# Moving VectorE's second operands into PSUM, two jobs to GpSimd, and a new order of jobs, in a one-core attention and mixture-of-experts kernel

## The reference

```python
xn = layernorm(x)
uv = silu(xn @ uv_w); u, v = split(uv)
s = (u * toeplitz_convolution(v, filter_from_a_small_network)) @ o_w
rw = softmax(mean over tokens of xn @ Wr + br)          # one row for each sequence
w, e = softmax(top_2(rw))                               # 2 of 8 experts for each sequence
out = sum_j w_j * (gelu(xn @ W1[e_j] + b1[e_j]) @ W2[e_j] + b2[e_j])
g = silu(layernorm(out + xn) * gamma + beta)
x = x + s * g
```

## Time and profile before

| | us |
|---|---|
| median of 3 runs | 209.76 (209.5 to 209.9) |
| profiled execution, time | 209.87 |
| profiled execution, span from first to last instruction | 207.9 |
| TensorE busy in the span | 180.2 (87%) |
| VectorE, ScalarE, GpSimd busy | 158.2, 126.2, 139.8 |

### The profile page before, as it was taken

One profiled execution on the slowest core, in us unless ns is written; L12 is line 12 of the kernel. 1 busy time (PEld: TensorE's weight loads), 2 busy tenths in 40 slices (PEclk: granted clock), 3 DMA queues, 4 the chain that ended last, 5 costly groups with the idle time before them and its releaser, 6 DMA issues.

```text
span 207.9 us, 3882 instructions
## 1 busy us (share of the span) xinstructions
PE 180.2 (87%) x1167; PEld 159.5 (77%) x1167; DVE 158.2 (76%) x430; ACT 126.2 (61%) x239; POOL 139.8 (67%) x144
## 2 busy tenths in 40 slices
PE   0747689999999999989999999999997989999661
PEld 0734378888899898858988888989885978899551
DVE  1685989779785289171997955699999968999694
ACT  1136628997999999969984647363147653453010
POOL 0402666566458494846579999999977995989500
PEclk9999559999999999999999999999999999999997
DMA  5535914604403103334323130010131011001103
GB/s 126 152 102 150 306 16 137 193 0 143 127 12 101 52 6 80 108 105 119 71 57 99 50 101 0 3 50 0 54 102 52 3 50 50 2 3 55 46 0 101
DMA packets 23212, 15.51 MB, mean 75 GB/s; under 512 B 1616, under 2 KB 20720, under 8 KB 23192
## 3 DMA queue, kind: packets, MB, share of 16 engines
q1 hardware_dynamic: 22816, 15.04, 25.2%
q10 hardware_dynamic: 376, 0.24, 0.7%
HBM read 13.17 MB, written 2.10 MB: 73 GB/s over the span
## 4 chain that ended last, share of the span: by engine, by line
PE 42%; DVE 25%; POOL 10%; issue 9%; ACT 8%; DMA 2%; SPq 1%; DVEq 0%; ACTq 0%; POOLq 0%
PE bank L1219 12%; PE bank L1057 6%; PE bank L1059 5%; PE bank L1058 5%; PE bank L1227 3%; DVE prod L933 3%; POOL Y L696 3%; PE bank L1123 3%; PE bank L1262 3%; DVE w_lo L779 2%; DVE x_all L1041 2%; POOL z_s L721 2%; DMA Y<-in_L_ffn_b 2%; ACT h_ring L580 2%; POOL prod L685 1%
## 5 line engine op out<-in xcount | busy, mean ns | idle before, releaser
L1219 PEld LDWEIGHTS bank<-w_s,h_ring 128*128 128x128 f32 x512 | 62.4, 192 | 2.4 <-issue 0.3
L1219 PE MATMUL bank<-w_s,h_ring 128*128 128x128 f32 x512 | 63.4, 275 | 0.1
L580 ACT ACTIVATE h_ring<-bank,b_sel 128x512 f32<-128x512 f32 x64 | 42.7, 686 | 19.7 <-PE bank L1059 11.8
L1057 PE MATMUL bank<-xT_hi,w_hi 128*128 128x512 f32 x64 | 30.4, 476 | 5.2 <-ACT h_ring L580 3.7
L1059 PE MATMUL bank<-xT_hi,w_lo 128*128 128x512 f32 x64 | 25.7, 402 | 0.0
L1058 PE MATMUL bank<-xT_lo,w_hi 128*128 128x512 f32 x64 | 25.6, 400 | 0.0
L696 POOL TENSOR_TENSOR Y<-prod 128x512 f32<-128x512 f32 x16 | 23.5, 1487 | 0.6
L930 DVE TENSOR_TENSOR prod<-bank,Qre 128x512 f32<-128x512 f32 x24 | 16.4, 684 | 5.4 <-POOL Y L696 4.9
L1057 PEld LDWEIGHTS bank<-xT_hi,w_hi 128*128 128x128 f32 x64 | 12.4, 193 | 8.8 <-ACT h_ring L580 5.2
L1262 PE MATMUL bank<-inv_sb,Y 128*128 128x128 f32 x128 | 16.0, 278 | 3.2 <-POOL Y L696 1.8
L1262 PEld LDWEIGHTS bank<-inv_sb,Y 128*128 128x128 f32 x128 | 15.1, 192 | 4.2 <-POOL Y L696 2.5
(11 more groups left out here) (155 smaller groups left out, 388.7 us busy)
## 6 DMA issues: line engine op xcount, KB each, us to landing
w_raw<-in_L_ffn_W SPq DMA_DIRECT2D x16, 256.0 KB, 2.7
w_s<-in_L_ffn_W SPq DMA_DIRECT2D x16, 256.0 KB, 2.8
x_all<-in_L_attn_x SPq DMA_DIRECT2D x8, 256.0 KB, 4.3
out_dram<-x_all SPq DMA_DIRECT2D x8, 256.0 KB, 2.3
b_in_sb<-in_L_ffn_b SPq DMA_DIRECT2D x16, 64.0 KB, 3.1
Y<-table_lag SPq DMA_DIRECT2D x1, 512.0 KB, 5.9
fwd_sb<-table_fwd SPq DMA_DIRECT2D x1, 256.0 KB, 3.8
inv_sb<-table_inv SPq DMA_DIRECT2D x1, 256.0 KB, 3.9
```

Of the source, the lines that this page charges most:

```text
L580: nc.scalar.activation(h_ring[:, n % NH], H_PS[n % 2][:], ACT.Gelu, bias=b1_sel[:, i, c:c + 1]).then_inc(h_done, 1)
L1057: nc.tensor.matmul(out_ps_ap, w_hi, m_hi, start=True, stop=False)
L1219: last = nc.tensor.matmul(OUT_PS[b % 2][:, tok], h_ring[:, n % NH, tok], w2_s[:, i % NW2, c], start=(n % HT == 0 and t == 0), stop=(n % HT ...
```

## The change

1. **Second operands in PSUM.** `y` (the experts' sum with xn) stays in its PSUM bank, and `ys`, `norm` and, for the last sequence, `aff` work on it there; tanh of the gate is written to the same bank, so that `g` reads it from PSUM and z from SBUF; `eo` writes both halves back into the PSUM bank, and `uc` reads them there; `sg` writes to PSUM, and `res` reads it there. So far each of `uc`, `g` and `res` read two operands from SBUF. The next-but-one sequence's first output block now waits for `g_done` where it waited for `y_done`.
2. **To GpSimd.** The lower part of W1 for all experts but the first, which is split on VectorE in 4 chunks as before (before, every second one), the lower part of uv_w, and the sum of the two b2 rows, which ScalarE scales both beforehand. From GpSimd to VectorE go the additions of epsilon and the negated means.
3. **To ScalarE.** The normalization of the second sequence, and the linear part of the filter network's silu (`lz`).
4. **Room.** `x_fold` lies in `uT`, one place for each sequence; 8 places for xT where there were 6; 4 for vt where there were 2. The last sequence's `back` and `s` go to the banks of `f0` and `f1`.
5. **Head.** Half of the first x is loaded on ScalarE's queue; one SyncE job fetches both experts of the first sequence; 33 matmuls `warm`, whose result nobody reads, stand between the first jobs of TensorE.
6. **Order.** All five tables are new.

```diff
-NXT, NRAW, NSPLIT, NW2, NH = 6, 3, 4, 4, 4
+NXT, NRAW, NSPLIT, NW2, NH, NV = 8, 3, 4, 4, 4, 4
+LO_ON = ["dve"] * 1 + ["pool"] * 15
 DVE_AT = {
-    "lo": [14, None, 27, None, 56, None, 60, None, 75, None, 86, None, 94, None, 106],
+    "lo": [13],
...
+            act_e.dma_start(x_all[:, 0, NT // 2:], x_v[0, :, NT // 2:]).then_inc(x0_in, 16)
             act_e.dma_start(c128[:], t_c128).then_inc(consts_in, 16)
...
+            def fetch_first(n):
+                sp.wait_ge(idx_done, 1)
+                e = []
+                for j in range(TOPK):
+                    e.append(sp.value_load(idx[0:1, 0, j:j + 1], min_val=0, max_val=E - 1))
+                    sp.dma_start(w1_raw[:, j, :], W1[bass.ds(e[j], 1), :, :]
+                                 .rearrange("e d f -> d (e f)")).then_inc(w1_in[j], 16)
...
-                nc.scalar.activation(lt, nrm, ACT.Tanh, bias=lnH[:, bias:bias + 1],
-                                     scale=lnH[:, scale:scale + 1]).then_inc(lt_done, 1)
+                nc.scalar.activation(A_PS[:, PW:2 * PW], nrm, ACT.Tanh, bias=lnH[:, bias:bias + 1],
+                                     scale=lnH[:, scale:scale + 1])
+                nc.scalar.activation(lz, nrm, ACT.Identity, bias=lnT[:, bias:bias + 1],
+                                     scale=lnT[:, scale:scale + 1]).then_inc(lt_done, 1)
...
+                step(nc.gpsimd.tensor_tensor(b2_mix[:, b % 2], b2_in_sb[:, b % 2, 0], b2_in_sb[:, b % 2, 1], ALU.add))
                 nc.gpsimd.tensor_tensor(xn[:, b], xn[:, b], bcast(b2_mix[:, b % 2].unsqueeze(1), [P, NT, D]),
-                                        ALU.add).then_inc(xb_pool, 1)
+                                        ALU.add).then_inc(xb_done, 1)
...
-                nc.vector.tensor_tensor(uT[:, b], uT[:, b], conv[:], ALU.mult).then_inc(uc_dve, 1)
+                u = uT[:, b].rearrange("p (k h n) -> p h k n", k=2, h=2)
+                nc.vector.tensor_tensor(u, u, EO_PS[b][:].rearrange("p (h k n) -> p h k n", k=2, h=2),
+                                        ALU.mult).then_inc(uc_done, 1)
...
-                nc.vector.tensor_tensor(flat(y_s[:, b % 2]), OUT_PS[b % 2][:], flat(xn[:, b]),
-                                        ALU.add).then_inc(y_done, 1)
+                nc.vector.tensor_tensor(OUT_PS[b % 2][:], OUT_PS[b % 2][:], flat(xn[:, b]), ALU.add).then_inc(y_done, 1)
...
-                nc.vector.tensor_tensor(g, S_PS[:], g, ALU.mult).then_inc(s_read, 1)
+                nc.vector.tensor_tensor(S_PS[b][:], S_PS[b][:], flat(th[:, b % 2]), ALU.mult).then_inc(sg_done, 1)
...
-                nc.vector.tensor_tensor(x_all[:, b], x_all[:, b], th[:, b % 2], ALU.add).then_inc(res_dve, 1)
+                nc.vector.tensor_tensor(x_b, S_PS[b][:], x_b, ALU.add).then_inc(res_done, 1)
...
                     if b >= 2:
-                        pe.wait_ge(y_done, b - 1)
+                        pe.wait_ge(g_done, b - 1)
...
+            def warm(n):
+
+                pe.wait_ge(set_done, 1)
+                nc.tensor.matmul(H_PS[1][:, 0:P], onesm, onesm, start=True, stop=True)
```

360 lines of the change are left out of this document (175 added, 185 removed), and 44 rows, old and new, of tables (ACT_AT, DVE_AT, PE_AT, POOL_AT).

## The result

The changed kernel takes 196.22 us (median of 4 executions, 194.88 to 200.85), the kernel before beside it on the same chip 209.83 us (4 executions, 209.5 to 211.03): a ratio of 0.932, with a 95% interval of 0.923 to 0.941. The prediction was 203.7 us with a range of 198 to 209. It had the sign right and was 7.5 us too slow.

What follows compares the result with a forecast made beforehand. TensorE bounds the middle; ScalarE comes next once the head shortens. 5.3 us less lost by TensorE plus 0.8 in the tail takes 6.1 off 209.87: 203.8, median 203.7, range 198 to 209.

Steps and rivals of the forecast that it cites:

- Head, order of the work: Head: W1's split no longer waits; first hidden block at 15.5 us instead of 20.34, first output block at 20.5.
- Head, warm: First mean in the head: warm matmuls keep TensorE going and save 0.9 us; bounds 0 or a loss of 1.
- The sign that I had named for a failure: Head: `warm` matmuls still running when the first mean's root is there would show the forecast wrong.
- With 13.8 + 5 + 3.5 TensorE has lost 22.3 at its last output block: Up to the last output block: TensorE loses 22.3 us, 5.3 less than before, so that block ends at 188.1 us.
- ScalarE is next: After the head: ScalarE's 37.0 us from first GELU to GELU 15 hold back hidden block 17; 13.8 us lost by then.
- The 5 for ScalarE's waits: Up to about GELU 28: ScalarE, without reserve, loses 5 us in waits; bounds 0 and 5.4 with 3 more.
- The second half's 3.5: From 96.4 to 193.4 us: the 3.5 us TensorE missed in the old profile were counted as lost again.
- PSUM operands: worth nothing directly: Middle: `res`, `g`, `uc` shrink by 11.3 us, but busy TensorE covers it; up to 8 us if TensorE waited.
- GpSimd's balance: First convolution sum to Y's end: 99.0 us, ending 2 us ahead of TensorE; as the bound, chance 0.15, kernel 207.2 us.
- Split moved to GpSimd: W1's lower parts: 7 moved splits cost GpSimd 8.9 us, at 1278 ns each against 691 on VectorE.
- Tail, 0.8 of 0 to 1.5: Tail: the last `back` no longer waits for its bank, saving 0.8 us within 0 to 1.5.
- Slower rival, the experts' bank held by `g`: Output blocks of sequence b+2 wait for `g` of b; kernel at 211 to 216 us; chance 0.11.

Runs made afterwards that it cites:

- the profile with the early head: Changed kernel with W1's lower parts 2, 4, ... 14 back on VectorE, alternating with GpSimd: 195.57 us, ratio 0.929 to the kernel before.
- the unedited kernel: The changed kernel timed again with nothing edited: 196.19 us, ratio 0.932 to the kernel before.
- the run with VectorE loaded: Changed kernel with 16 extra 128x512 SBUF copies on VectorE, about 95 to 165 us, output unused: 202.95 us, ratio 0.964 to the kernel before.

## Why the prediction was wrong, by its own steps

For the median the 13.6 us divide into 3.3 in the middle (158.1 against 161.4), 0.4 to 1.3 in the tail, and by difference some 9.4 in the head, which puts its first output block at about 22.6 us; the profiles have it between 21.2 and 26.7. The prediction had 11.5, 0.8, and a middle that was 6.2 us longer (188.1 - 20.5 = 167.6 us). The head was 2 us too good, the middle 9.5 us too bad.

- **Head, order of the work: right.** First hidden block at 16.1 us and first output block at 21.2 in an execution with an early full rate, forecast 15.5 and 20.5; chunks of 0.28 us; the upper part no longer waits. That the order of the split is what wins it is read from the rows: no run puts the split back alone, or takes away the second queue for x or the joint fetch.
- **Head, warm (0.9 us won, bounds 0 and a loss of 1): right in size for the median, partly by luck.** Without warm the kernel is 1.1 us slower, with intervals that overlap. I had warm keep TensorE at full rate in the first mean. In fact it is a bet: it pays 2 us when full level comes by 6 us (21.2 against 23.3 for the first output block) and costs up to 3.4 when it comes at 16 or 17 us (26.7). The sign that I had named for a failure, warm still running when the first mean's root is there, stands in the profile, and the kernel was faster all the same.
- **"With 13.8 + 5 + 3.5 TensorE has lost 22.3 at its last output block": the step that failed.** "ScalarE is next" was right. But I had TensorE lose 10.5 us behind the first output block: 2 ahead of hidden block 17, "I take 5" for ScalarE's waits, and the second half's 3.5. The traces show 2.3 us of idle time. That is 8.2 of the 9.5 us; the other 1.3 is TensorE's work in the middle (155.8 measured, 157.1 in the forecast's count).
- **The 5 for ScalarE's waits.** In the profile with the early head GELU 15 ends at 59.3 us, 39.9 us behind the first. ScalarE works for 38.5 of them, where I had 37.0: its unit prices were 1.5 us too low, and its waits are 1.3 us (0.6 in the unedited kernel). TensorE's count ahead of block 17, which starts at 59.4, was 2.5 us too low (34.8 us of work from 22.2 us on, for 32.3; 1.9 too low in the unedited kernel), and behind it 3.2 us too high (120.7 for 123.9). With all the 5 us ahead of it block 17 would have started at 60.7, so the errors nearly cancel up to there. The waits between 33 and 97 us of before were, as I now read them, those of an engine with reserve. That a load on ScalarE costs 0.6 to 0.8 of itself says that it has next to none now.
- **"The second half's 3.5": carried over without asking what caused them.** They are zero now. The row gave the idle time, not its releaser; the trace has it, as shown above (1.54 us for a GELU, 1.07 for Y, 0.74 for VectorE). So the larger part of the miss lies behind block 17: 3.5 of carried waits and 3.2 of TensorE's count. That stretch is where the operands act: with them back in SBUF it is 2.9 us longer. It does not bring back the same waits, so which part of the change removed each of them is not shown.
- **"PSUM operands: worth nothing directly": wrong.** The 11.3 us less on VectorE were sized well (0.69, 0.68 and 0.68 us each), the 3.2 on GpSimd too low: at 1.28 us each its sums take 6.1 us less in all (51.2 for 57.3). TensorE as a cover was the error: a busy TensorE hides nothing if its own next block waits for VectorE's chain (`p1` to `f0`, `uc` to `back`), as in the run with VectorE loaded. An added microsecond on VectorE costs 0.37 to 0.45 there. The Trainium skill, SBUF — State Buffer, section "Who interferes with whom", has VectorE instructions with two SBUF inputs contend with GpSimd's reads, and these runs agree: 1.05 against 0.69 us for `res`, and 1.38 against 1.28 for GpSimd's sums.
- **GpSimd's balance, 2 us ahead of TensorE: the gap is right, its terms are not.** It is 1.4 us ahead. But from its first convolution sum (90.7 us) to Y's end (182.8) are 92.1 us in the unedited kernel, not 99.0; TensorE ended early by about as much, so the agreement is luck. 4.9 us more cost 1.05 in the middle; as a rival it did not come true.
- **Split moved to GpSimd: no gain and no loss.** Undone it changes nothing beyond the interval.
- **Tail, 0.8 of 0 to 1.5: right**, 0.4 to 1.3.
- **Slower rival, the experts' bank held by `g`: it never shows**; no output block waits for `g` in any profile.

The range failed with the middle: its lower end of 198 took 0 for ScalarE's waits and still held the 3.5 us of the second half.

What stays open: when TensorE reaches its full rate. I can name the times of the profiles (4.1 to 5.4, 9.5, 15.9 and 17.3 us with the 33 warm matmuls, 4.0 to 6.9 with 36 or 41, 13.5 and 16.3 with 23, 17.4 without), and that the times with 36 and 41 spread less, not what picks among them in one execution. Open too is how the head's 9.4 us divide among the order, the loads and warm.
